# The scan stage of a two-layer Perceiver kernel: row spreading moved from DMA to TensorE, two products moved from VectorE to GpSimd

## The reference

```
delta  = clip(softplus(dt_raw @ W_dt.T + b_dt), 1e-4, 1)
b_term = tanh(b_raw);  c_term = tanh(c_raw)            # [token, 8]
a      = softplus(A_log) + 1e-4                        # [channel, 8]
decay  = clip(exp(-delta[..., None] * a), 1e-4, 1)     # [token, channel, 8]
drive  = (1 - decay) * (b_term[:, :, None, :] * xb[..., None])
state  = decay * state + drive                         # token after token
y      = sum(state * c_term, -1) + D * xb
out    = concat([y, zb]) @ W_out.T
```

## Time and profile before

| | us |
|---|---|
| three runs | 3904.15, 3909.54, 3909.21 |
| median | 3909.21 |
| the profiled execution, its own time | 3904.15 |
| its span | 3902.8 |
| mean granted clock of TensorE | 0.954 |

### The profile page before, as it was taken

The page is one execution under the profiler, slowest core; times in us unless marked ns, Lnnn a source line. Parts: engine busy times, 40 slices in busy tenths (PEclk is TensorE's granted clock), DMA queues, the critical chain, the costliest instruction groups (busy, mean ns, idle before and its releaser), DMA issues. The chain is left out here.

```text
span 3902.8 us, 46028 instructions
## 1 busy us (share of the span) xinstructions
PE 3611.3 (93%) x17868; PEld 2318.5 (59%) x17868; DVE 2529.3 (65%) x3462; ACT 1920.9 (49%) x1962; POOL 1776.0 (46%) x744
## 2 busy tenths in 40 slices
PE   6999899989999999986797999999999887799997
PEld 5777688755555555432674455555554375588886
DVE  2222234347777777637796877777776464699997
ACT  2111211145555555642683456555656321577785
POOL 1111111149999999920000599999998320100000
PEclk8999999999999999996897799999999998799999
DMA  6455655553333333102686233333331101799996
GB/s 254 162 185 186 204 174 174 180 154 87 87 74 85 87 87 82 51 23 106 263 356 215 56 85 87 87 85 81 88 87 30 49 1 48 276 370 373 376 380 252
DMA packets 215944, 593.83 MB, mean 152 GB/s; under 512 B 42624, under 2 KB 108192, under 8 KB 161840
## 3 DMA queue, kind: packets, MB, share of 16 engines
q1 hardware_dynamic: 176944, 517.47, 40.8%
q10 hardware_dynamic: 36864, 67.13, 4.6%
q0 software_dynamic: 1920, 6.29, 0.5%
HBM read 470.64 MB, written 120.09 MB: 151 GB/s over the span
## 5 line engine op out<-in xcount | busy, mean ns | idle before, releaser
L636 DVE TENSOR_REDUCE maxima<-psum 128x1 f32<-128x512 f32 x2048 | 1290.4, 682 | 387.7 <-PE psum L631 384.1
L745 ACT ACTIVATE pt<-psum 128x1024 f32<-128x1024 f32 x1024 | 1019.3, 1025 | 702.9 <-PE psum L656 697.7
L759 POOL TENSOR_TENSOR exp_sums<-pt 128x1024 f32<-128x1024 f32 x342 | 818.6, 2394 | 266.0 <-PE psum L672 132.8
L631 PE MATMUL psum<-ks,first_q 96*128 96x512 f32 x2048 | 814.5, 447 | 19.7 <-DMA first_q<-q_parts 8.4
L762 POOL TENSOR_TENSOR exp_sums<-exp_sums,pt 128x1024 f32<-128x1024 f32 x310 | 737.3, 2378 | 45.8 <-ACT pt L745 1.5
L668 PE MATMUL psum<-pt,vs 128*32 128x512 f32 x4096 | 675.5, 599 | 4.6 <-DVE head_rows L772 2.2
L631 PEld LDWEIGHTS psum<-ks,first_q 96*128 96x128 f32 x2048 | 394.0, 192 | 477.7 <-DVE maxima L636 321.2
L672 PE MATMUL psum<-exp_sums,constants 128*32 128x512 f32 x1408 | 671.3, 599 | 0.0
L656 PE MATMUL psum<-qs,ks 97*128 97x512 f32 x2048 | 649.8, 400 | 15.1 <-ACT pt L745 15.1
L1422 DVE TENSOR_TENSOR moe_cut<-moe_raw,moe_cut 128x2048 fp32r<-128x2048 f32 x244 | 557.1, 2291 | 57.7 <-ACT moe_cut L1364 52.7
L1364 ACT CAST moe_cut<-moe_raw 128x2048 fp32r<-128x2048 f32 x244 | 467.2, 1921 | 64.9 <-PE psum L97 64.9
(11 more groups left out here) (310 smaller groups left out, 4395.9 us busy)
## 6 DMA issues: line engine op xcount, KB each, us to landing
moe_raw<-in_moe_w SPq DMA_DIRECT2D x244, 1024.0 KB, 7.8
ks<-k_parts SPq DMA_DIRECT2D x384, 256.0 KB, 4.6
k_parts<-kparts ACTq DMA_DIRECT2D x256, 256.0 KB, 2.9
cx<-in_ctx SPq DMA_DIRECT2D x32, 1024.0 KB
v_heads<-vrow SPq DMA_DIRECT2D x32, 1024.0 KB, 5.8
vs<-v_heads SPq DMA_DIRECT2D x32, 1024.0 KB, 5.3
first_q<-q_parts SPq DMA_DIRECT2D x96, 64.0 KB, 4.0
qs<-q_parts SPq DMA_DIRECT2D x96, 64.0 KB, 4.9
```

What stands on the lines that cost most here:

```text
L631: pe.matmul(self.c.bank[self.FIRST_BANK + k % 3], self.first_q[s][:, t * P:(t + 1) * P], self.ks[s][part][0:3 * DH, at:at + CHUNK], start= ...
L636: dve.tensor_reduce(self.maxima[:, h % 2, i % TT, i // TT:i // TT + 1], self.c.bank[self.FIRST_BANK + k % 3], X, ALU.max).then_inc(*self.f ...
L745: act.activation(self.pt[:, self.slot(h, b) + i:self.slot(h, b) + i + 2, :], self.c.psum[:, at:at + 2, :], ACT.Exp).then_inc(*self.exp.up())
L759: engine.tensor_tensor(to, self.pt[:, slot:slot + R, :], self.pt[:, slot + R:slot + 2 * R, :], ALU.add).then_inc(*signal.up())
```

## The change

The rows are no longer spread by DMA. TensorE multiplies a 0/1 matrix (`pick`, already among the constants), 8 rows by 128 columns with ones in row s, by `bc`, which puts row s on all partitions, in bank 0 for b and bank 1 for c. ScalarE copies both to `terms`. It goes one state at a time, two states ahead of the loop; since banks 0 and 1 held dt before, TensorE waits until VectorE has clipped delta. The tanh of b keeps its sign, so `drive` needs 1 - decay: a new VectorE instruction makes it (into the new tile `rest`). The products of b row and xb and of state and c row go to GpSimd, which gets a list of its own (`on_pool`). The look-ahead `prepare` on VectorE is gone: each step's four instructions stand behind each other, each with a wait for the one before.

```diff
     STEPS = DSTATE * CB
 
-    def __init__(self, c, A, S, x):
-        self.c, self.A, self.S, self.x = c, A, S, x
+    def __init__(self, c, A, x):
+        self.c, self.A, self.x = c, A, x
...
             self.decay = c.sb(st, "decay", [P, self.RING, TOK])
+            self.rest = c.sb(st, "one_minus_decay", [P, self.RING, TOK])
...
-            self.decayed, = c.signals(st, "decayed")
-            self.bc_out, self.term_in = c.landings(st, "bc_out_0 bc_out_1"), c.landings(st, "term_in_0 term_in_1")
+            self.spread_made, self.spread, self.decayed, self.driven = c.signals(st, "spread_made spread decayed driven")
...
             self.on_pe(c.pe)
+            self.on_pool(c.pool)
...
-        for which in range(2):
-            sp.wait_ge(*self.bc_done.at(which + 1))
-            sp.dma_start(self.S["bc"][which], self.bc[:, which, :]).then_inc(*self.bc_out[which].up())
-        for which in range(2):
-            sp.wait_ge(*self.bc_out[which].at(1))
-            sp.dma_start(self.terms[:, which], self.S["bc"][which].rearrange("s n -> (s n)").partition_broadcast(P).rearrange("p (s n) -> p s n", s=DSTATE)).then_inc(*self.term_in[which].up())
...
         pe.wait_ge(*self.bc_done.at(2))
         pe.wait_ge(*self.w_out_in.at(1))
+        pe.wait_ge(*self.clipped.at(CB + 1))
+
+        def spread_terms(s):
+            for which in range(2):
+                if s:
+                    pe.wait_ge(*self.spread.at(2 * (s - 1) + which + 1))
+                pe.matmul(bank[which], c.pick[0:DSTATE, s * P:(s + 1) * P], self.bc[:, which, :], start=True, stop=True).then_inc(*self.spread_made.up())
...
+        spread_terms(0)
+        spread_terms(1)
         pe.wait_ge(*self.silued.at(KD))
         for t in range(TT):
             output_part(t, range(CB, KD))
         for i in range(self.STEPS):
+            if i % CB == 0 and i // CB + 2 < DSTATE:
+                spread_terms(i // CB + 2)
             if i:
                 add(i - 1)
         add(self.STEPS - 1)
...
-            act.activation(self.bc[:, which, :], bank[5 + which][0:DSTATE, :], ACT.Tanh, scale=(-1.0, 1.0)[which]).then_inc(*self.bc_done.up())
+            act.activation(self.bc[:, which, :], bank[5 + which][0:DSTATE, :], ACT.Tanh).then_inc(*self.bc_done.up())
...
+                act.wait_ge(*self.spread_made.at(2 * s + which + 1))
+                act.copy(self.terms[:, which, s, :], bank[which]).then_inc(*self.spread.up())
...
+        decays(0)
+        spread_terms(1)
         for i in range(self.STEPS):
-            decays(i)
+            if i + 1 < self.STEPS:
+                decays(i + 1)
+            if i % CB == 0 and i // CB + 2 < DSTATE:
+                spread_terms(i // CB + 2)
...
-        def prepare(i):
-
+        for i in range(self.STEPS):
             r = i % self.RING
             dve.wait_ge(*self.decayed.at(i + 1))
             dve.tensor_scalar(self.decay[:, r, :], self.decay[:, r, :], 1e-4, 1.0, ALU.max, ALU.min).then_inc(*self.step.up())
-            dve.tensor_tensor(self.drive[:, r, :], self.terms[:, 0, i // CB, :], self.conv[:, i % CB, :], ALU.mult).then_inc(*self.step.up())
+            dve.wait_ge(*self.step.at(3 * i + 1))
+            dve.tensor_scalar(self.rest[:, r, :], self.decay[:, r, :], -1.0, 1.0, ALU.mult, ALU.add).then_inc(*self.step.up())
             dve.wait_ge(*self.step.at(3 * i + 2))
-            dve.scalar_tensor_tensor(self.drive[:, r, :], self.decay[:, r, :], 1.0, self.drive[:, r, :], ALU.subtract, ALU.mult).then_inc(*self.step.up())
-
-        dve.wait_ge(*self.silued.at(KD))
-        dve.wait_ge(*self.term_in[0].at(1))
-        prepare(0)
-        prepare(1)
-        for i in range(self.STEPS):
-            r = i % self.RING
+            dve.wait_ge(*self.driven.at(i + 1))
+            dve.tensor_tensor(self.drive[:, r, :], self.rest[:, r, :], self.drive[:, r, :], ALU.mult).then_inc(*self.step.up())
             dve.wait_ge(*self.step.at(3 * i + 3))
+            if i >= self.RING:
+                dve.wait_ge(*self.weighed.at(i - self.RING + 1))
             dve.tensor_tensor_scan(self.state[:, r, :], self.decay[:, r, :], self.drive[:, r, :], 0.0, ALU.mult, ALU.add).then_inc(*self.scanned.up())
...
-            if i + 2 < self.STEPS:
-                prepare(i + 2)
-            if i == 0:
-                dve.wait_ge(*self.term_in[1].at(1))
-            if i >= self.RING:
-                dve.wait_ge(*self.added.at(i - self.RING + 1))
-            dve.wait_ge(*self.scanned.at(i + 1))
-            dve.tensor_tensor(self.part[:, r, :], self.state[:, r, :], self.terms[:, 1, i // CB, :], ALU.mult).then_inc(*self.weighed.up())
...
+    def on_pool(self, pool):
+        CB, RING = self.CB, self.RING
+        pool.wait_ge(*self.silued.at(KD))
+
+        def drive(i):
+            if i >= RING:
+                pool.wait_ge(*self.scanned.at(i - RING + 1))
+            pool.wait_ge(*self.spread.at(2 * (i // CB) + 1))
+            pool.tensor_tensor(self.drive[:, i % RING, :], self.terms[:, 0, i // CB, :], self.conv[:, i % CB, :], ALU.mult).then_inc(*self.driven.up())
+
+        def weigh(i):
+            pool.wait_ge(*self.scanned.at(i + 1))
+            pool.wait_ge(*self.spread.at(2 * (i // CB) + 2))
+            if i >= RING:
+                pool.wait_ge(*self.added.at(i - RING + 1))
+            pool.tensor_tensor(self.part[:, i % RING, :], self.state[:, i % RING, :], self.terms[:, 1, i // CB, :], ALU.mult).then_inc(*self.weighed.up())
+
+        drive(0)
+        for i in range(self.STEPS):
+            if i + 1 < self.STEPS:
+                drive(i + 1)
+            if i:
+                weigh(i - 1)
+        weigh(self.STEPS - 1)
...
-            "bc": nc.dram_tensor("bc_rows", [2, DSTATE, TOK], F32, kind="Internal").ap(),
```

More of the change, by code:

```diff
@@ L1941, in perceiver @@
             attention.run()
-        SelectiveScan(c, A, scratch, x).run()
+        SelectiveScan(c, A, x).run()
         Experts(c, A, scratch, x, 0).run()
```

1 line of the change is left out of this document (added).

## The result

The changed kernel takes 3935.73 us (median of 6 runs, 3932.28 to 3937.34), the kernel before 3907.89 (6 runs, 3901.43 to 3909.54). The ratio is 1.0075, with a 95% interval of 1.0062 to 1.0087: 24 to 34 us slower. The record has three more runs of the changed kernel, 3936.99, 3938.07 and the profiled one, 3938.72; with them its median would be 3936.47. The forecast was 3934, in a range of 3919 to 3946.

The account below looks back on a forecast made before the run. VectorE's instruction list was taken to bound the scan stage, 3.38 us a step. The terms +4.9, +19.4, +0.2, +0.9 and +1.2 sum to +26.6, giving 3930.8 or 3935.8 us by starting run; forecast 3934, range 3919 to 3946.

Parts of the forecast that it names:

- start, to the first scan's end: From the rates to the first scan's end: waiting for TensorE's spreading, ScalarE's copies and the table load costs +4.9 us.
- fifteen more steps: Scan loop after the first scan: 68.6 us instead of 49.25, +19.4, with thirteen steps at 4.66.
- last weighting: After the last scan: the weighting takes 1.27 + 0.05 us on GpSimd in place of 1.16, +0.2.
- last sum: Last sum on TensorE after the loop: 2.08 us instead of 1.13 as its work is thin, +0.9.
- second output part: TensorE's output part after the loop: partly at 1.2 GHz, between 0.5 and 2.3 us more, taken as +1.2.
- Removing the transfers is worth nothing: Before the scan: the DMA transfers of B and C rows were already covered, so removing them gains nothing.
- GpSimd and VectorE exclude each other; period 4.66: Scan loop: products on GpSimd alternate with VectorE's instructions, making a step 4.66 us against 3.38.
- The last two steps 3.70: End of the scan loop: two steps with no drive product to let in take 3.70 us each.
- The third decay stalls by 0.6 us: Third step: its decay stands behind copies of the third pair, these behind TensorE's output part, adding 0.6 us.
- Rival 2: First output part: TensorE stays at 1.2 GHz throughout, delaying the third decay; +8.4 us on the sum, 3942; chance 0.14.
- Rival 1: Scan loop: GpSimd runs beside VectorE without exclusion, 2.75 us a step; +2.5 us, 3912; chance 0.09.
- Rival 3: Scan loop: only part of VectorE's work is held, period 4.08 us; 7.5 less, 3927; chance 0.12.

Follow-up runs that it names:

- c: The changed kernel with the rows spread by DMA as before, so only the products move to GpSimd; 3929.88 us, 1.0064 of the kernel before.
- a: The changed kernel with both products moved back from GpSimd to VectorE; 3925.37 us, 1.0050 of the kernel before.
- e: The changed kernel with GpSimd's two products a step replaced by memsets to a constant; one run, 3917.67 us beside 3911.86.
- g: Against c, decays in two PSUM banks, fused subtract and multiply back, sign of b turned as before; 3897.37 us, 0.9980 of the kernel before.
- d: The changed kernel with ScalarE's first three decays ahead of the first copies, later decays ahead of copies; 3935.91 us, 1.0073 of the kernel before.
- f: The changed kernel with the spreading products made over 128 rows instead of 8; 3935.48 us, 1.0071 of the kernel before.
- b: The kernel before with only the spreading moved to TensorE and ScalarE, products and look-ahead staying on VectorE; 3932.0 us, 1.0065 of before.

## Why the prediction was right

The terms, in us, worked out and in the profiled executions:

| term | forecast | measured |
|---|---|---|
| start, to the first scan's end | +4.9 | +5.0 |
| fifteen more steps | +19.4 | +21.65 |
| last weighting | +0.2 | +0.2 |
| last sum | +0.9 | +0.95 |
| second output part | +1.2 | +2.4 |
| stage | +26.6 | +30.1 |

- *Removing the transfers is worth nothing.* Right: c has them and differs from the changed kernel only by the start and the third decay, both of which the removal brought.
- *GpSimd and VectorE exclude each other; period 4.66.* Right in mechanism and size: 4.65 in the changed kernel and in c. Shown from three sides: taking GpSimd's work away shortens the step although VectorE has more (a), letting it write only frees the product (e), and taking the decay out of SBUF frees all (g). The period came out to 0.01 because no scan has a GpSimd product beside it in this order, as the prediction said; d shows what it costs when one has.
- *The last two steps 3.70.* 3.70 and 3.72.
- *The third decay stalls by 0.6 us.* This is the step that was mis-sized: it was 3.0. I had let the clock come back by 1775 (1778 in the changed kernel's times), 4.4 us after the spreading began as in the earlier trace rows. It stayed at 0.50 until after 1785, so the second pair and the first 4 us and more of the output part ran at 1.2 GHz. The output part began 7.2 us after the rates instead of 6.0 and took 9.44 instead of 7.13, and VectorE waited 4.80 for the clip instead of 1.2. The sum has a slip too: 1776.6 and 7.13 are 1783.7, not 1783.4. Rival 2, that it stays down through the whole output part, had 8.4 for this; the truth was between. f shows that the 8 rows of the spreading products made the difference: with 128 rows the step took 5.03.
- *The second output part +1.2.* It was 2.4, just past the upper end that I had written (2.3): the granted clock was 0.50 from 1859.4 to 1864.0 and 1.00 from 1864.5, so of the 9.51 us the first 4.6 at least ran at 1.2 GHz.
- *Rival 1, no exclusion:* refuted by the period of 4.65 in the changed kernel and in c, and by a. *Rival 3, tensor_scalar free:* refuted by one minus decay at 1.37.

The total agrees better than the stage does, and that part is luck. The sum was 26.6 for a stage that took 30.1 more; but between the medians there are only 27.8, and the kernel before came out at 3907.89 instead of the 3909.21 from which the forecast started. Executions differ by several us outside the stage; d shows how much that can be. The forecast of 3934 against the first three runs' median of 3909.21 is a difference of 24.8; against the 27.8 measured, it was 3 us short.

## What to carry to other kernels

Work does not get out of the way by moving it to an engine that has to take turns with the first: before a product goes from VectorE to GpSimd, look for a place in the trace where both run instructions of that kind and compare their ends, not their lengths. If the move is wanted, give VectorE's instructions at most one SBUF input first, by leaving one operand in a PSUM bank, and keep a tensor_scalar from having both ends in SBUF; here that turned a step of 4.65 us into one of 2.57 with the same work on GpSimd. And an order written by hand that puts another engine's slow results ahead of what the bounding engine needs next costs a wait each time it comes round (b), which a second, larger loss can hide.

## What the runs showed of the hardware that I had not expected

- TensorE busy without a gap for 7.1 us with products of 8 rows left the granted clock at 0.50; the same products over 128 rows, most of them zeros, had it up after less than 5 us (f).
- The scan takes turns with GpSimd's products in both directions: a product issued during a scan took 2.01 us and ended 1.06 after it, and a scan issued during a product took 2.17 instead of 1.22 (d). In PSUM the decay leaves it one SBUF input, and beside GpSimd's product it takes 1.22 (g).
- A memset on GpSimd lengthens a single-input VectorE instruction with both ends in SBUF (0.71 for 0.40) and not a two-input product beside it (0.69) (e).
- A clip of 128x512 within PSUM takes 0.67 us against 0.40 in SBUF; the scan takes 1.22 from either.
- In one profiled execution the clock was lower in a stage some 1400 us behind the change, 0.74 for 1.00, worth 6 us, as much as the effect that was to be measured (d).
